# Second layer of the experts' later blocks as three f32r products of high and low parts

## What is computed

```python
logits = flat_x @ W_router + b_router
top_vals, top_idx = jax.lax.top_k(logits, 2)
...
for e in range(8):
    h = relu(flat_x @ W1[e] + b1[e])      # 256 -> 1024
    y = h @ W2[e] + b2[e]                 # 1024 -> 256, the second layer
    final_output += y * w[:, None]        # w: the token's weight for e
```

## Time and profile before

| what | us |
|---|---|
| median of three runs (lowest, highest) | 1715.55 (1706.52, 1716.07) |
| the profiled execution | 1717.18 |
| its span, first to last instruction | 1715.3 |
| PE busy in it | 1629.1 (95%) |
| DVE, ACT, POOL busy | 1025.0, 788.5, 323.5 |
| mean granted TensorE clock | 0.979 |

### The profile page before, as it was taken

The page is one execution under the profiler, slowest core; times in us unless marked ns, Lnnn a source line. Parts: engine busy times, 40 slices in busy tenths (PEclk is TensorE's granted clock), DMA queues, the critical chain, the costliest instruction groups (busy, mean ns, idle before and its releaser), DMA issues.

```text
span 1715.3 us, 29817 instructions
## 1 busy us (share of the span) xinstructions
PE 1629.1 (95%) x10070; PEld 978.8 (57%) x10070; DVE 1025.0 (60%) x2366; ACT 788.5 (46%) x1635; POOL 323.5 (19%) x310
## 2 busy tenths in 40 slices
PE   4889999999999999999999999979999999999996
PEld 2433343344454444444443443359999889998986
DVE  4688777888777778777788774324344323333322
ACT  2136656667546666645666657732221212221221
POOL 6201120002100140210031100332144121222121
PEclk9799999999999999999999999989999999999999
DMA  6920441243140440342440621144566756666663
GB/s 171 181 64 26 77 78 18 25 65 42 39 77 26 78 79 11 34 72 66 65 68 25 139 84 66 60 154 135 154 192 182 206 164 177 185 167 174 184 159 73
DMA packets 92661, 173.31 MB, mean 101 GB/s; under 512 B 13235, under 2 KB 51123, under 8 KB 92384
## 3 DMA queue, kind: packets, MB, share of 16 engines
q1 hardware_dynamic: 75376, 143.69, 33.9%
q0 software_dynamic: 15744, 26.54, 7.4%
q10 hardware_dynamic: 1392, 1.18, 0.3%
HBM read 133.69 MB, written 37.29 MB: 100 GB/s over the span
## 4 chain that ended last, share of the span: by engine, by line
PE 88%; DVE 3%; ACT 3%; DMA 2%; issue 2%; POOL 1%; ACTq 0%; SPq 0%; DVEq 0%; POOLq 0%
PE ps L1014 15%; PE ps L1221 14%; PE ps L1203 14%; PE ps L1040 14%; PE ps L1000 13%; PE ps L1070 3%; DVE rmax L1370 2%; PE ps L1079 2%; ACT prob L1233 2%; PE ps L1123 2%; PE ps L1092 2%; PE ps L1061 2%; PE ps L1003 2%; PE ps L1043 2%; PE ps L1191 1%
## 5 line engine op out<-in xcount | busy, mean ns | idle before, releaser
L1370 DVE TENSOR_REDUCE rmax<-ps 128x1 f32<-128x512 f32 x1024 | 664.7, 686 | 212.3 <-PE ps L1040 106.8
L1233 ACT ACTIVATE prob<-ps 128x512 f32<-128x512 f32 x1024 | 562.6, 600 | 347.2 <-PE ps L1003 183.9
L1040 PE MATMUL ps<-stacked_k,stacked_q 112*128 112x512 bf16 x1024 | 394.5, 390 | 17.0 <-DVE rmax L1370 8.9
L1000 PE MATMUL ps<-stacked_q,stacked_k 115*128 115x512 bf16 x1024 | 361.0, 384 | 7.9 <-ACT prob L1233 5.4
L1014 PE MATMUL ps<-prob,values 128*32 128x512 f32 x2048 | 275.4, 610 | 7.0 <-ACT prob L1233 6.5
L1221 PE MATMUL ps<-w,hidT 128*128 x1136 | 260.3, 382 | 9.3 <-issue 7.4
L1203 PEld LDWEIGHTS ps<-xiT,w_now 128*128 128x128 f32 x2272 | 266.9, 193 | 3.7
L1203 PE MATMUL ps<-xiT,w_now 128*128 128x128 f32 x2272 | 268.6, 276 | 0.0
L1040 PEld LDWEIGHTS ps<-stacked_k,stacked_q 112*128 112x128 bf16 x1024 | 100.0, 98 | 294.0 <-DVE rmax L1370 204.1
L1339 ACT ACTIVATE hidT<-ps,b 128x128 f32<-128x128 f32 x284 | 81.3, 369 | 359.7 <-PE ps L1203 338.8
L1221 PEld LDWEIGHTS ps<-w,hidT 128*128 128x128 f32 x1136 | 210.1, 190 | 42.6 <-issue 16.4
(11 more groups left out here) (181 smaller groups left out, 1158.4 us busy)
## 6 DMA issues: line engine op xcount, KB each, us to landing
w_now<-in_w SPq DMA_DIRECT2D x71, 1024.0 KB
stacked_q<-parts_of_rows SPq DMA_DIRECT2D x90, 128.0 KB, 6.7
stacked_k<-parts_of_rows SPq DMA_DIRECT2D x90, 128.0 KB, 7.4
xi<-expert_rows SPq DMA_DIRECT2D x71, 130.0 KB
w<-in_w SPq DMA_DIRECT2D x8, 1024.0 KB, 9.3
parts_of_rows<-q_part SPq DMA_DIRECT2D x21, 256.0 KB, 7.9
parts_of_rows<-k_part SPq DMA_DIRECT2D x21, 256.0 KB, 7.9
xr<-in_x POOLq DMA_DIRECT2D x4, 1024.0 KB, 9.3
```

The costliest lines, as they stand in the source:

```text
L1000: m = e.matmul(ps[:, bank, :], ka[i][0:ROWS, hh, kt * P:(kt + 1) * P], qa[i][0:ROWS, hh, ch * BANK:(ch + 1) * BANK], start=True, stop=True)
L1040: m = e.matmul(ps[:, bank, :], qa[i][0:MAX_ROW, hh, qt * P:(qt + 1) * P], ka[i][0:MAX_ROW, hh, kc * BANK:(kc + 1) * BANK], start=True, sto ...
L1233: e.activation(prob[:, u % NPROB, :], ps[:, u % NSCORE, :], ACT.Exp).then_inc(sem["exp"], 1)
L1370: e.tensor_reduce(rmax[:, G % 2, hh * NT + qt, kc:kc + 1], ps[:, p.bank("max", *k), :], AX.X, ALU.max).then_inc(sem["maxed"], 1)
```

## The change

For blocks 40 to 70 the second layer h @ W2 is computed as high(h) high(W2) + high(h) low(W2) + low(h) high(W2). High is the value rounded to f32r, a 4-byte type that TensorE multiplies in another mode than f32; low is what is left, value minus high, as f32r too. Per block these steps come in:
- `hid_high`, per half (ACT): a copy of four chunks of `hidT`, 128x512, to `hid_high`.
- `hid_low`, per half (DVE): `hidT` minus `hid_high`, 128x512.
- `w2_high` (ACT): a copy of the expert's 128x2048 weights to `w2_high`, for the block two ahead, behind the `down` that frees the buffer.
- `w2_low` (DVE and POOL): `w2` minus `w2_high`, six of eight chunks (128x1536) on DVE, two (128x512) on POOL.

`down` becomes `down_in_parts`: 24 products of 256 columns on fixed tiles, without `value_load`. It waits for both `w2_low` and, per half, for `hid_low`.

```diff
+DVE_CHUNKS = 3 * FC // 4
@@ blocks
                 for half in range(2):
                     up_half(n + 1, half)
+                    if n + 1 >= EARLY:
+                        add("hid_high", n + 1, half)
+                        add("hid_low", n + 1, half)
                     yield
@@
             add("added", n)
+            if EARLY <= n + 2 < NBLK:
+                assert ("zeros", NE - 1) in p.number
+                add("w2_high", n + 2)
+                add("w2_low", n + 2)
@@ build
+            w2_high, w2_low = ([sb(f"w2_{n}{i}", [P, FC, D], F32R) for i in range(2)] for n in ("high", "low"))
+            hid_high, hid_low = ([sb(f"hid_{n}{i}", [P, FC, P], F32R) for i in range(2)] for n in ("high", "low"))
@@ tensor
+            def down_in_parts(n, bank):
+
+                m = n - EARLY
+                e.wait_ge(sem["w2_low"], m + 1)
+                e.wait_ge(sem["w2_low_pool"], m + 1)
+                for c in range(FC):
+                    if c % (FC // 2) == 0:
+                        e.wait_ge(sem["hid_low"], 2 * m + 1 + c // (FC // 2))
+                    products = ((hid_high, w2_high), (hid_high, w2_low), (hid_low, w2_high))
+                    for i, (rows, weights) in enumerate(products):
+                        last = e.matmul(ps[:, bank, 0:D], rows[n % 2][:, c, :], weights[n % 2][:, c, :],
+                                        start=(c == 0 and i == 0), stop=(c == FC - 1 and i == 2))
+                last.then_inc(sem["down"], 1)
@@ scalar
+                elif kind == "hid_high":
...
+                    e.wait_ge(sem[("hid_fore", "hid_aft")[half]], n + 1)
+                    e.activation(hid_high[n % 2][:, chunks, :], hidT[n % 2][:, chunks, :], ACT.Copy).then_inc(sem["hid_high"], 1)
+                elif kind == "w2_high":
...
+                    elif n >= EARLY + 2:
+                        e.wait_ge(sem["down"], n - 1)
+                    expert = e.value_load(expert_of[0:1, n:n + 1], min_val=0, max_val=NE - 1)
+                    e.activation(w2_high[n % 2][:, :, :], second_layer(expert, slice(0, FC)), ACT.Copy).then_inc(sem["w2_high"], 1)
@@ vector
+                elif kind == "hid_low":
...
+                    e.tensor_tensor(hid_low[n % 2][:, chunks, :], hidT[n % 2][:, chunks, :], hid_high[n % 2][:, chunks, :].bitcast(F32),
+                                    ALU.subtract).then_inc(sem["hid_low"], 1)
@@ gpsimd
+                elif kind == "w2_low":
+                    n, = k
+                    chunks = slice(DVE_CHUNKS, FC)
...
+                    expert = e.value_load(expert_of[0:1, n:n + 1], min_val=0, max_val=NE - 1)
+                    e.wait_ge(sem["w2_high"], p.upto("w2_high", n))
+                    e.tensor_tensor(w2_low[n % 2][:, chunks, :], second_layer(expert, chunks), w2_high[n % 2][:, chunks, :].bitcast(F32),
+                                    ALU.subtract).then_inc(sem["w2_low_pool"], 1)
```

More of the change, by code:

```diff
@@ L79 @@
     "act": {"exp": 0.61, "av": 0.61, "turned": 0.61, "high": 0.7, "norm": 0.55, "cross_exp": 0.9, "p_turned": 0.55, "weigh_exp": 0.35,
[L80 removed]
+            "c_turned": 0.45, "kv_made": 0.5, "qk_made": 0.5, "cb_made": 0.4, "cv_made": 0.45, "xi_turned": 0.4, "hid_fore": 1.5,
+            "hid_high": 0.6, "w2_high": 1.95},
     "dve": {"maxed": 0.67, "nmax": 0.3, "nrow": 1.7, "on": 0.75, "stats": 0.42, "aggr": 0.9, "shift": 0.25, "rest": 0.78, "values": 0.9,
             "add1": 0.72, "add2": 0.72, "cross_max": 1.0, "cross_norm": 1.9, "logits_made": 1.8, "second": 1.2, "weigh": 0.2,
[L83 removed]
+            "chosen": 0.25, "ranked": 2.0, "slots": 1.7, "rows": 1.4, "table": 1.0, "hid_aft": 1.4, "yo": 1.2, "hid_low": 0.65, "w2_low": 1.8},
     "pool": {"rstd": 1.75, "mid": 0.63, "low": 1.2, "bias1": 0.7, "bias2": 0.7, "scatter": 1.3, "added": 1.6, "fetch": 0.9},
@@ L1212, in _ @@
                         e.wait_ge(sem["yo"], n)
[L1213 to L1223, removed]
+                    if n >= EARLY:
+                        down_in_parts(n, AV_BANK)
+                    else:
+                        if n == 0:
+                            e.wait_ge(sem["table"], p.upto("table", 0, TABLE_PARTS - 1))
+                        expert = e.value_load(expert_of[0:1, n:n + 1], min_val=0, max_val=NE - 1)
+                        for c in range(FC):
+                            if c == 0:
+                                e.wait_ge(sem["hid_fore"], n + 1)
+                            elif c == FC // 2:
+                                e.wait_ge(sem["hid_aft"], n + 1)
+                            m = e.matmul(ps[:, AV_BANK, 0:D], hidT[n % 2][:, c, :], w2[:, bass.ds(expert, 1), c, :].rearrange("p a f -> p (a f)"),
+                                         start=(c == 0), stop=(c == FC - 1))
+                        m.then_inc(sem["down"], 1)
         @block.scalar
@@ L1617, in _ @@
                     m.then_inc(sem["hid_aft"], 1)
+                elif kind == "hid_low":
+                    n, half = k
+                    chunks = slice(half * FC // 2, (half + 1) * FC // 2)
+                    e.wait_ge(sem["hid_high"], p.upto("hid_high", n, half))
+                    if half == 0 and n >= EARLY + 2:
+                        e.wait_ge(sem["down"], n - 1)
+                    e.tensor_tensor(hid_low[n % 2][:, chunks, :], hidT[n % 2][:, chunks, :], hid_high[n % 2][:, chunks, :].bitcast(F32),
+                                    ALU.subtract).then_inc(sem["hid_low"], 1)
+                elif kind == "w2_low":
+                    n, = k
+                    chunks = slice(0, DVE_CHUNKS)
+                    expert = e.value_load(expert_of[0:1, n:n + 1], min_val=0, max_val=NE - 1)
+                    e.wait_ge(sem["w2_high"], p.upto("w2_high", n))
+                    e.tensor_tensor(w2_low[n % 2][:, chunks, :], second_layer(expert, chunks), w2_high[n % 2][:, chunks, :].bitcast(F32),
+                                    ALU.subtract).then_inc(sem["w2_low"], 1)
                 elif kind == "yo":
@@ L1701, in _ @@
                                          xn[:, tt, :], None).then_inc(sem["scattered"], 16)
+                elif kind == "w2_low":
+                    n, = k
+                    chunks = slice(DVE_CHUNKS, FC)
+                    if n == EARLY:
+                        e.wait_ge(sem["table"], p.upto("table", 1, TABLE_PARTS - 1))
+                    expert = e.value_load(expert_of[0:1, n:n + 1], min_val=0, max_val=NE - 1)
+                    e.wait_ge(sem["w2_high"], p.upto("w2_high", n))
+                    e.tensor_tensor(w2_low[n % 2][:, chunks, :], second_layer(expert, chunks), w2_high[n % 2][:, chunks, :].bitcast(F32),
+                                    ALU.subtract).then_inc(sem["w2_low_pool"], 1)
                 elif kind == "added":
```

11 lines of the change are left out of this document (added).

## The result

| | before | after |
|---|---|---|
| median of the runs | 1713.01 us (1704.13 to 1717.05, 12 runs) | 1723.4 us (1714.71 to 1730.59, 12 runs) |
| ratio, 95% interval | | 1.006 (1.0033 to 1.0087) |
| profiled execution, its span | 1717.18, 1715.3 | 1730.59, 1728.8 |
| first layer of block 40 starts | 1464.40 | 1467.76 |
| period of blocks 40 to 70 | 7.570 | 7.803 |

The forecast was 12 us faster; the change makes the kernel 10 us slower, by 0.6%. Of the 13.4 us between the two profiled executions 3.4 lie before block 40, where nothing was changed: that start wanders between 1453.6 and 1467.8 in the profiled executions of this case, so it is chance. The 30 periods bring 7.0 and the end 3.1, 10.1 together; the medians lie 10.4 apart.

The account below looks back on a forecast made before the run. TensorE (88% of the span) was taken to bound, then a loop over ACT and DVE at 7.2 us a block; 11.1 us saved over 30 blocks and 1.0 at the end took 1717.2 to 1705.1; forecast 1705, range 1699 to 1737.

Parts of the forecast that it names:

- preparation does not run ahead there: On POOL's queue: the register load waits for the DMA's issue, since indirect DMAs stand 0.30 us apart, so nothing is lost.
- blocked port: Rival, chance 0.31: POOL's subtraction takes the SBUF port before DVE's low part; period 8.15 us, time 1733 us.
- margin of 0.2 to 0.3: Between DVE's low part issued at 2.4 us behind yo and POOL ready at 2.6; called thin.
- 0.49: Chance given to the main case: the loop at about 7.2 us a block without a blocked port.
- 8.15 a block: Period in us forecast for blocks where POOL's subtraction holds up DVE's low part; +16 us, 1733 in all.
- 0.8 us of slack: On TensorE, per block: slack beside the loop, said to cover its own "issue" stalls, which add 0.32 us a block.
- loop of about 7.2: Row of ACT and DVE steps up to the next first layer: a block every 7.2 us instead of 7.57.
- the additions fit beside it only just: Other added ACT and DVE steps end by T+9.2 and T+11.1, needed at 9.28 and 11.1; no slack left.
- One pass for a product: On TensorE: an f32r product of 256 columns costs 0.11 us, so 24 take 2.6 and a block 6.4.
- The last second layer starts after yo as now and is 1.0 shorter.: At the kernel's end, behind the last first layer: 1.0 us saved.

Follow-up runs that it names:

- e3: Changed kernel with all eight chunks of w2's low part subtracted on DVE and none on POOL; 1716.0 us, 1.0024 of the kernel before.
- e5: Kernel before the change, with the first-layer weight loads of blocks 43 to 70 cut from 1 MB to 8 KB; 1700.8 us.
- e2: Changed kernel with w2's low part split four chunks to DVE and four to POOL, instead of six and two; 1755.2 us.
- e1: Changed kernel with one more wait: POOL's subtraction starts only behind DVE's hid_low of the block's first half; 1712.6 us, 1.0008 of the kernel before.
- e4: Changed kernel splitting only blocks 40 and 41, whose parts the later blocks multiply again; 1700.3 us, 0.9923 of the kernel before.
- e10: Changed kernel, reordered: DVE does hid_aft before both hid_low, ACT copies xiT before the second hid_high; whole loads; 1710.7 us, 1.0004 of the kernel before.
- e7: Changed kernel with POOL's subtraction waiting behind hid_low and first-layer weight loads of blocks 43 to 70 cut from 1 MB to 8 KB; 1703.8 us.
- e11: Changed kernel with DVE's hid_aft before both hid_low, ACT's xiT before the second hid_high, each weight load as four DMAs; 1697.4 us, 0.9947 of the kernel before.
- e12: Kernel before the change, with each 1 MB first-layer weight load issued as four DMAs; 1708.7 us, 1.0003 of the uncut kernel.

## Why the prediction was wrong

**Where it broke: "preparation does not run ahead there".** The blocked port was my first rival, and I had named what decides it: whether POOL's register load runs while its DMA is still being prepared. I argued that it does not, from indirect DMAs that stand 0.30 apart. The row of line 1778 settles it:

```profile
L1778 POOLq TENSOR_LOAD <-expert_of x2: 289/290/292, 1562.3 to 1570.3; - x2
```

The load runs at 1562.3, *before* the DMA begins at 1562.57, and the subtraction can start as soon as the DMA is through. Two instructions of one kind in a row showed that a DMA is not prepared while another is; they said nothing of a register load behind one. The evidence was of another kind of instruction than the claim, and with a margin of 0.2 to 0.3 I should not have put 0.49 on one side of it. From there the rival went as written: DVE's large subtraction to 1564.36, then POOL's to 1565.50, then `hid_low` to 1566.04. The Trainium skill has this in SBUF — State Buffer, section SBUF: two separate sides: GpSimd reading SBUF and DVE with two SBUF inputs lock each other out. The runs agree, with 1.59 against 0.69 us here, at most 694 ns without POOL (e3), and up to 3.04 us for a double share.

**The rival's price was too high**: 8.15 a block, where the mean was 7.80 and 7.66 the typical one; nine of the 30 took 8.0 to 8.5. Take the typical one. I had `hid_low` end 4.3 behind yo's end; it ended 3.75 behind (1562.29 to 1566.04). DVE's large subtraction ended 0.2 earlier than I had it, and `hid_low` came 0.54 behind POOL's end, not 0.77. The rest was gained on ACT: `xiT` began 0.10 before `hid_high` had ended by its record, and the next first product came 0.05 behind `xiT` and not 0.25.

**The second break: what bounded before.** "What remains is that 0.8 us of slack now covers TensorE's own 'issue' stalls." They were not TensorE's own; with the short landings of e5 they are gone. What TensorE waited for does not stand in its "issue" rows, and two queues have to be read for it. SP waits for the landing too, before it loads the rows `xi` of a later block (L970: us in total, times, longest, between 1464 and 1692). Then one block, in order of time:

```profile
SPq L970 <- DMA out<-yo,xi: 158.8, 30, 6.4
...
1546.45 0.48 DVE L1630 SCALAR_TENSOR_TENSOR yo<-ps,weight,bias 128x256 f32<-128x256 f32 x1 [1.63 <-PE ps L1221]
1547.64 0.34 SPq L971 DMA_DIRECT2D xi<-expert_rows  x1
1548.95 0.19 SPq L967 DMA_DIRECT2D w_now<-in_w  x1
...
L1189 PEldq EVENT_SEMAPHORE  x1: 51/51/51, 1549.8 to 1549.8; - x1
L1215 PEldq TENSOR_LOAD <-expert_of x1: 414/414/414, 1549.9 to 1549.9; - x1
...
1550.83 0.91 PE L1221 MATMUL ps<-w,hidT 128*128 x3 [0.51 <-issue]
```

By the semaphore events an output DMA landed at 1546.91. SP issued the load of the rows 0.73 later, they landed at 1549.78, and 0.03 behind that TensorE's queue got past its wait for them (L1189), which stands ahead of the second layer's register load (L1215). So that load came late, and the second layer with it. In each of the blocks 44 to 68 this wait ended 0.03 us behind the landing of the rows. The last `yo` had ended at 1546.93, 3.0 before the register load, so TensorE did not wait for it. The weights' load (L967) stands behind the rows on the same queue, and so is issued just when the next output DMA is under way, where e2 has it 3.0 us ahead of one and a landing of 3.99.

The restarts show the other half: 10 of 22 at the floor, where a landing of 6.78 and 0.71 alone make 7.49 a block. With whole loads no version came far under it: e1, e3, e4 and e10 lie between 7.35 and 7.61. The profile showed it, had I asked: a queue whose every entry waits for the one before (line 1713) has a period of its own, landing and restart, and I had looked at POOL's row only for its start. "Idle before <-DVE yo" on it named the wait that came last, in a wait for two.

**What held.** The loop of about 7.2 (e7: 7.22, in part by luck as said above), and that the additions fit beside it only just. One pass for a product: 0.12 us for 256 columns where I had 0.11, so 2.87 for the 24 where I had 2.6; TensorE's block is 6.66 and not 6.4. Of the sizes, ACT's 0.63 and 1.91 and DVE's 0.69 and 1.79 were right within 0.05, ACT's 1.91 at the upper end of what I gave (DVE's is 1.76 where POOL stays away); POOL's subtraction alone took 1.29 where I had 1.16.

**The third, small break: the end.** "The last second layer starts after yo as now and is 1.0 shorter." It starts after yo, but yo of block 69 now comes behind two `hid_low` and a blocked one among them, so TensorE idles 3.2 us ahead of it where it idled 1.5 before. The windows of that stretch (columns as above):

```profile
1709.00:1711.80 2.80, 0.01 (x1) 0.01 (x1) 1.91 (x5) 0.55 (x1) 0.00 (x0) 0.81 0.00 0
1711.80:1717.40 5.60, 5.48 (x24) 5.18 (x24) 1.02 (x4) 0.00 (x0) 1.55 (x1) 0.50 0.22 26
```

The granted clock is 0.50 (1.2 GHz) behind that pause, and the 24 products take 5.5 us and not 2.87. Before, it stayed at 1.00 over the shorter pause. The end cost 3.1 us in this execution, and it was priced at -1.0. The length of the pause does not decide it alone: in e1 TensorE paused 3.2 us too and the clock behind it was 1.00 (24 products in 2.9 us, end 25.4), in e10 it was 1.00 behind 2.3 us, and in e11 0.63 behind as much (4.6 us for the 24). What else decides stays open, and so does how often the kernel after pays for it.

**Still open.** Why a landing beside the same load varies between blocks, why a load issued just behind the DMA delays it so, and what of it each of the 16 engines holds up, was not tried; nor was the wait on `added` itself, since without it two DMAs could add to one row at a time.

## What to carry to other kernels

Before you price what a change takes from the busiest engine, look for a queue in which each entry waits for the landing of the one before it: its landing and restart are a period of their own, and may stand a few tenths over the engine's. Look also for what else waits for that landing: here SP's queue did, and through it TensorE. Three bounds stood within 0.4 us of each other here: DMAs at 7.4 to 7.6 in both kernels, TensorE at 7.25 before, the new loop at 7.2 after. Products alone (e4, with most of the splitting left out) brought 0.8%, the new order alone (e10) and the pieces alone (e12) nothing that the times show, and both together with the products (e11) 0.5%. And where a sharing of work decides by 0.2 us who takes a port first, write the order down with a wait, which brought back 0.22 us a block here.

## What the runs showed of the hardware that was not expected

- POOL's queue loads a register ahead of a DMA that has not begun: at 1562.33, for a DMA at 1562.57, though it stands behind it in the program.
- A DVE subtraction of 128x512 that meets POOL's ends 0.54 us behind POOL's end, and its record is longer by the wait (1.59 to 1.79); POOL's own record is 1.91 where it is 1.29 in e1. It begins while DVE's large subtraction runs (to 1564.36) and ends 1.14 behind that one's end, so part of it is taken to be waiting. A long record thus need not be a slow operation.
- An output DMA of 128 rows that adds in memory lands in 3.9 us with loads of 8 KB, in 6.3 to 6.8 where a 1 MB load in runs of 4 KB is mostly issued 0 to 1.3 us behind its start, and in 3.99 where that load is issued 3.0 us ahead of it (e2). With the load as four DMAs in runs of 1 KB, whose issues spread over 1.7 us, it is 5.6 to 5.7; whether the runs or the moments make the difference was not tested. The next one begins 0.71 us behind the landing at the soonest, where it begins 0.28 behind the end of a `yo` on DVE.
- f32r products of 256 columns follow each other every 0.12 us; the f32 ones took 0.43 each.
